# The weights stage of a graph kernel: part of the one-hot work moved to GpSimd

## What is computed

```python
    alpha = leaky_relu(s_src[row] + s_dst[col], 0.2)
    m = maximum(segment_max(alpha, row), 0.0)
    ex = exp(alpha - m[row])
    denom = segment_sum(ex, row) + (E - deg)[:, None] * exp(-m)
    alpha_n = ex / denom[row]
    msg = alpha_n[:, :, None] * h[col]
    out = segment_sum(msg, col, num_segments=N).reshape(N, H * C) + bias
```

## Time and profile before

| | us |
|---|---|
| median of 3 runs | 5210.12 (5208.03 to 5211.01) |
| profiled execution | 5210.29 |
| its span, first to last instruction | 5208.5 |
| weights stage in it, about | 2488 to 2986 |

### The profile page before, as it was taken

How to read it: one execution, slowest core, us unless ns; L and a number is a source line. 1 busy time by engine, 2 the same in 40 slices (tenths; PEclk the granted TensorE clock), 3 DMA queues, 4 the chain that set the end, 5 groups by cost and what they waited for, 6 DMA issues and landing times. The chain is left out here.

```text
span 5208.5 us, 102749 instructions
## 1 busy us (share of the span) xinstructions
PE 3975.9 (76%) x26030; PEld 3300.0 (63%) x26031; DVE 3727.5 (72%) x8186; ACT 3056.9 (59%) x4419; POOL 3139.4 (60%) x3290
## 2 busy tenths in 40 slices
PE   6887888888888888500899977777777777777778
PEld 5776666667666666400788836666666666666666
DVE  9866666666666666449999957777777777777777
ACT  3455555555555455302999966666666666666665
POOL 0277777777777777730000027777777777777774
PEclk9998988988889898755999989999999999999999
DMA  9855555555555544492200086666666666666665
GB/s 388 275 144 130 131 131 132 132 130 132 131 132 132 132 131 133 137 74 8 60 0 0 11 209 146 146 146 145 146 145 146 145 146 145 147 145 146 145 146 135
DMA packets 1157485, 695.20 MB, mean 133 GB/s; under 512 B 923562, under 2 KB 974948, under 8 KB 1157324
## 3 DMA queue, kind: packets, MB, share of 16 engines
q1 hardware_dynamic: 807980, 307.66, 30.5%
q0 software_dynamic: 131424, 275.52, 18.1%
q10 hardware_dynamic: 218048, 111.65, 7.4%
HBM read 542.65 MB, written 145.42 MB: 132 GB/s over the span
## 5 line engine op out<-in xcount | busy, mean ns | idle before, releaser
L1162 POOL DMA_INDIRECT g_q<-q_d,g_aux x1660 | 1571.2, 947 | 1311.0 <-DMA pw<-g_q 805.5
L614 POOL DMA_INDIRECT rec_d<-rec,place x1568 | 1514.6, 966 | 490.8 <-issue 475.9
L1488 PE MATMUL g_hp<-pw,g_mix 128*128 x3328 | 875.9, 386 | 316.2 <-ACT g_mix L1384 310.9
L1499 PE MATMUL g_ap<-g_hid,g_oh 128*128 128x256 f32 x3328 | 876.6, 386 | 137.0 <-DVE agg L1286 131.8
L721 PE MATMUL lk<-tab_sd,low 128*128 128x196 f32 x3136 | 980.2, 397 | 0.0
L1404 ACT ACTIVATE g_hid<-g_q 128x512 f32<-128x512 f32 x832 | 524.0, 630 | 711.1 <-DVE g_q L1272 699.0
L1272 DVE TENSOR_TENSOR g_q<-g_hp,g_q 128x512 f32<-128x512 f32 x832 | 573.8, 690 | 484.4 <-DMA g_q<-q_d,g_aux 350.3
L1488 PEld LDWEIGHTS g_hp<-pw,g_mix 128*128 128x128 f32 x3328 | 616.0, 190 | 473.9 <-issue 398.5
L593 ACT ACTIVATE equal<-rk,minus_two 128x512 bf16<-128x512 f32 x392 | 258.7, 685 | 944.7 <-DMA rec_d<-rec,place 724.0
L1499 PEld LDWEIGHTS g_ap<-g_hid,g_oh 128*128 128x128 f32 x3328 | 595.7, 190 | 286.4 <-issue 219.9
L1286 DVE TENSOR_TENSOR agg<-agg,g_ap 128x256 f32 x1664 | 691.4, 415 | 100.6 <-PE g_ap L1499 38.9
(11 more groups left out here) (265 smaller groups left out, 5164.9 us busy)
## 6 DMA issues: line engine op xcount, KB each, us to landing
low_row<-rows_d SPq DMA_DIRECT2D x392, 256.0 KB
g_ea<-rec_d SPq DMA_DIRECT2D x208, 256.0 KB, 4.6
rec<-in_ea ACTq DMA_DIRECT2D x196, 256.0 KB
rec_d<-pad ACTq DMA_DIRECT2D x49, 936.0 KB, 6.7
hx_row<-rows_d SPq DMA_DIRECT2D x392, 98.0 KB
g_lrow<-low_row_d SPq DMA_DIRECT2D x208, 128.0 KB, 4.4
g_q<-q_d,g_aux POOLq DMA_INDIRECT x1660, 3.0
rec_d<-rec,place POOLq DMA_INDIRECT x1568
```

The lines of the kernel that those rows point to most:

```text
L614: pool.indirect_dma_start(rec_d, bass.IndirectOffsetOnAxis(ap=place[0:n, at, j:j + 1], axis=0), rec[0:n, at, j, :], None).then_inc(s_sc[at ...
L1162: pool.indirect_dma_start(qg[:, par, j, :], None, q_d, bass.IndirectOffsetOnAxis(ap=aux[:, par, j, F_IDX - F_LOW:REC - F_LOW].bitcast(I32) ...
L1488: mm = pe.matmul(hp[u][:, k * HID:(k + 1) * HID], mix[:, par, 2 * u + k, :], pw[:, bass.ds(b[k], 1), :].rearrange("p o f -> p (o f)"), sta ...
L1499: mm = pe.matmul(ap[u % 2][:, k * HID:(k + 1) * HID], oh[:, par, 2 * u + k, :], hid[:, u, k, :], start=True, stop=True)
```

## The change

GpSimd gets a loop in the weights stage. For each group it subtracts, for tiles 0 to 4 (`AWAY = 5`), the high digit from the numbers 0 to 195, in one operation of 5 x 196 elements that writes the difference into `oh_high`. ScalarE then takes the absolute value in place, in one operation without a bias over the five tiles, and then max(0, 1 - x) as before, over five tiles instead of four. VectorE compares tiles 5 to 7 (`COMPARED = 3`). TensorE starts with those three tiles. The wait for a free buffer moves from ScalarE to GpSimd, and ScalarE waits for GpSimd's new semaphore `d_pool`.

```diff
+AWAY, COMPARED = 5, 3
...
-        high_two = halved_bf[:, S:2 * S].rearrange("p (g j s) -> p g j s", j=HG, s=2)
+        high_two = halved_bf[:, S:S + S // G * COMPARED * 2].rearrange("p (g j s) -> p g j s", j=COMPARED, s=2)
...
-                        act.activation(high_two[:, gs, :, :], by_group[:, :, HG:G].unsqueeze(3).to_broadcast([P, SC // G, HG, 2]),
+                        act.activation(high_two[:, gs, :, :], by_group[:, :, AWAY:G].unsqueeze(3).to_broadcast([P, SC // G, COMPARED, 2]),
                                        ACT.Copy).then_inc(s_ld, 1)
...
             @block.gpsimd
             def _(pool):
+                def away(g, at):
+                    if not first(g, 4):
+                        pool.wait_ge(d_acc, g - 3)
+                    pool.tensor_tensor(oh_high[:, at, 0:AWAY, :], row(high_of, P, AWAY, NQ),
+                                       col(high_dst[:, bass.ds(g * G, AWAY)], P, AWAY, NQ), ALU.subtract).then_inc(d_pool, 1)
+
+                pool.wait_ge(s_const, 1)
+                quads(pool, away, NGS)
...
-                    v.tensor_tensor(oh_high[:, at, HG:G, :].rearrange("p j (a s) -> p j a s", s=2),
-                                    high_two[:, bass.ds(g, 1), :, :].rearrange("p o j s -> p (o j) s").unsqueeze(2)
-                                    .to_broadcast([P, HG, NQ // 2, 2]),
-                                    high_of.rearrange("p (a s) -> p a s", s=2).unsqueeze(1).to_broadcast([P, HG, NQ // 2, 2]),
-                                    ALU.is_equal)
+                    to = [P, COMPARED, NQ // 2, 2]
+                    v.tensor_tensor(oh_high[:, at, AWAY:G, :].rearrange("p j (a s) -> p j a s", s=2),
+                                    high_two[:, bass.ds(g, 1), :, :].rearrange("p o j s -> p (o j) s").unsqueeze(2).to_broadcast(to),
+                                    high_of.rearrange("p (a s) -> p a s", s=2).unsqueeze(1).to_broadcast(to), ALU.is_equal)
...
                 def turned_low(g, at):
-                    if not first(g, 4):
-                        act.wait_ge(d_acc, g - 3)
-                    for j in range(HG):
-                        ins = act.activation(oh_high[:, at, j, :], high_of, ACT.Abs, bias=high_dst[:, bass.ds(g * G + j, 1)], scale=-1.0)
-                    ins.then_inc(d_dist, 1)
+                    act.wait_ge(d_pool, g + 1)
+                    to = oh_high[:, at, 0:AWAY, :].rearrange("p j a -> p (j a)")
+                    act.activation(to, to, ACT.Abs).then_inc(d_dist, 1)
                     act.wait_ge(d_dist, g + 1)
-                    act.activation(oh_high[:, at, 0:HG, :], oh_high[:, at, 0:HG, :], ACT.Relu, bias=ones[:, 0:1], scale=-1.0
-                                   ).then_inc(d_lo, 1)
+                    act.activation(to, to, ACT.Relu, bias=ones[:, 0:1], scale=-1.0).then_inc(d_lo, 1)
...
-                    for j in [*range(HG, G), *range(HG)]:
+                    for j in [*range(AWAY, G), *range(AWAY)]:
```

More of the change, by code:

```diff
@@ L1086, in build @@
             d_hi, d_w, d_acc = sem("e_high_ready"), sem("e_weights_ready"), sem("e_multiplied")
+            d_pool = sem("e_differences_ready")
             d_dist, d_lo = sem("e_distances_ready"), sem("e_low_ready")
@@ L1438, in weighted @@
                             mm = pe.matmul(acc[:, 0:NQ], spread[:, at, k * HEADS:(k + 1) * HEADS, :, j].rearrange("p h q -> p (h q)"),
-                                           oh_high[:, at, j, :], start=first(g) and j == HG and k == 0,
-                                           stop=isinstance(g, int) and g == NGS - 1 and j == HG - 1 and k == THREE - 1,
+                                           oh_high[:, at, j, :], start=first(g) and j == AWAY and k == 0,
+                                           stop=isinstance(g, int) and g == NGS - 1 and j == AWAY - 1 and k == THREE - 1,
                                            skip_group_check=True)
```

## The result

The changed kernel took 5522.12 us (median of 4 runs, 5521.01 to 5523.64) against 5210.57 us for the kernel before (4 runs): a ratio of 1.0597, 95% interval 1.0585 to 1.0610.

What follows compares the result with a forecast made beforehand. ScalarE was taken to bound the weights stage at 2.38 us a group, VectorE close behind. Turns of 2.25 plus 2.13 us make 4.38 us, over 208 groups +416 us on 5210: 5626 us, range 5180 to 5760 us.

Steps and rivals of the forecast that it cites:

- What bounds: Weights stage before the change: 208 groups of 2.38 us, bound by ScalarE, with VectorE only 0.03 us behind.
- the sum: Weights stage: VectorE's 2.25 us plus GpSimd's 2.13 us make 4.38 us a group, +416 us, 5626 us.
- the likeliest case: Weights stage: VectorE's three operations and GpSimd's subtraction take turns by whole instructions, 4.38 us a group, 5626 us; chance 0.55.
- The mechanism: Weights stage: VectorE operations with two SBUF inputs and GpSimd's SBUF-reading subtraction share a read interface, each holding the other.
- GpSimd's price: Subtraction of 980 elements a group: 2.13 us, bounded by 0.90 us (one pass) and 2.53 us (three passes).
- The two-pass value: GpSimd's subtraction if the write runs beside its two reads: 1.72 us a group.
- The turnovers: Two handovers of 0.12 us a group between VectorE and GpSimd, counted only in the upper bound of 5.02 us.
- TensorE's clock: Weights stage: TensorE, idle half the time, may be granted 1.2 GHz and need 4.14 us, still under 4.38 us.
- A: Weights stage: VectorE and GpSimd run side by side, VectorE binds at 2.25 us a group, 5183 us; chance 0.22.
- B: Weights stage: side by side, but the subtraction alone takes 2.53 us, over 2.38 us; +31 us, 5241 us; chance 0.05.
- C: Weights stage: turns shorter than an instruction hide about half the subtraction, 3.32 us a group, 5406 us; chance 0.15.
- The signs it named: Stage timeline: large product or its neighbours about 2.1 us longer once a group, period near 4.4 us; otherwise product unchanged, 2.25 us.

Runs made afterwards that it cites:

- the write-only experiment: The changed kernel with GpSimd's subtraction replaced by a memset of the same 980 elements a group, which reads nothing and leaves the weights out: 5182.68 us.

## Why the prediction was right, point by point

*What bounds.* Right. ScalarE was relieved as worked out: 1021 and 1112 ns against 1.02 and 1.12 us. VectorE's compare takes 467 instead of 593 ns, and its three operations without company 2.25 us a group, as the sum had it; the write-only experiment and the last two groups of the stage both show 2.25. GpSimd's turn came on top, as the likeliest case said.

*The mechanism.* Right, and narrower than the rows of before could tell. In the earlier trace rows the two engines hold one another to the end of an instruction; in the earlier trace rows an addition with two SBUF inputs runs undisturbed inside an indirect DMA of GpSimd. The experiments show that a GpSimd memset doesn't touch VectorE's operations with two SBUF inputs and that an operation that reads SBUF does; the addition of the earlier trace rows would fit if that DMA's operation reads no SBUF in this way, which no run shows. Why the copy of the earlier trace rows, with one input, is held was not tried. The conversion that lasted 5.43 us beside a memset is a second such row: an operation of VectorE with one input can be held too, which the turns found here don't cover. *SBUF — State Buffer* of the Trainium skill, section "Who interferes with whom", says just that of VectorE operations with two SBUF inputs. The runs agree with it in the three ways that were tried: beside memsets the three operations kept 1.75, 0.28 and 0.46 us, beside a reading operation the 256-element compare took 1085 ns, and compares with one SBUF input were not held (0.41 and 0.75 us).

*The mis-sized term.* The step that was off is GpSimd's price, taken as 2.13 us, the middle between two and three passes at the rate of a memset. What a group paid is 1.63 us by the periods (3.88 less 2.25 us) and 1.60 us by the compare's length. That is two passes: alone the whole subtraction takes 1.83 us, which leaves no room for a third pass of 0.81 us behind the reads, so the write runs beside them; and 0.23 us of the operation run beside VectorE, so that no fixed part is paid. The difference, 2.13 less 1.63 us, is 0.50 us a group; times 208 that is 104 us, the whole gap between 5626 and 5522 us. The two-pass value that the prediction listed, 1.72 us, would have given 2.25 + 1.72 = 3.97 us a group and about 5541 us. *GPSIMD Engine Reference* of the Trainium skill, section 3.1, led to an estimate of 2.15 us for the operation; its figure is for an addition of float32 numbers. Alone the subtraction measured 1.83 us here, with bf16 and float32 inputs and a bf16 output, and the measurement decides.

*The turnovers* of 0.12 us, put into the range alone, were not paid on top: 2.25 and 1.60 us are 3.85 of the period's 3.88 us. The 0.14 us by which the held compare outlasts the subtraction lie within the 0.28 us that it needs anyway.

*TensorE's clock.* It was granted 1.00, the upper level of 2.4 GHz, in the stretch shown although TensorE was idle for 1.80 us in each group, and the 24 loads kept their 2.07 us. The 4.14 us that the prediction estimated for 1.2 GHz did not come up; they would have bound, since the period is 3.88 us.

*The rivals.* A (side by side, 5183 us) would have needed the subtraction to leave the compares alone; its time is what a GpSimd operation without reads gives, 5182.68 us. B falls with the 1.83 us, which is under 2.38 us. C (half of it hidden, 3.32 us a group) falls with the period of 3.88 us, of which only 0.23 of 1.83 us are hidden, and with the lengths: a compare of 0.28 us waits out 1.6 us of reads, while the product ahead of it is not stretched at all.

*The signs it named.* Two of them were badly chosen. The large product's length was to decide between the likeliest case and A, and the prediction was to be wrong if the product kept its length while a subtraction ran beside it. In the plain stretch it does keep it, 1.75 us, and only at the stage's start one product took 3.37 us. Still the two take turns there: the subtraction starts after the product and waits for it, 3.06 us where it takes 1.83 us alone. By that sign alone the result would have been read as A, or as a miss. What tells the cases apart is the length of the product's neighbour, 1893 ns, which the prediction named too, and the period. The second poor sign is the range: 5180 to 5760 us reaches from a faster kernel to one that is 550 us slower, so that a time inside it says little; the case's own range, 5370 to 5759 us, says more. The other condition was met: the price lies between 0.90 and 2.53 us.

Neither the changed kernel nor the one with its numbers in PSUM, the two that still compute the weights, beats the kernel before. An element that GpSimd reads costs VectorE 0.81 ns, and the subtraction reads two for each; a compare on VectorE costs 0.53 ns an element. So a tile that VectorE gives up gives back 0.10 us and takes 0.32 us (196 x 2 x 0.81 ns), and the four tiles that came from ScalarE give VectorE nothing back. By this estimate, which rests on two and on five tiles, the move loses for any number of tiles, as long as all of VectorE's operations read two streams of SBUF.

## What to carry to other kernels

Before work is moved to an idle GpSimd, look at what VectorE runs meanwhile: where its operations have two inputs in SBUF and no gaps, every element that GpSimd reads is paid in VectorE's time (0.81 ns each here), so that the move pays only if it frees more than that, even if GpSimd has nothing else to do. What GpSimd only wrote cost such operations nothing here, but a memset held a VectorE conversion with one input for its whole 5.33 us, so that writing is not free in general. An engine whose smallest, unchanged operation suddenly takes six times as long, with the end of another engine's instruction just ahead of its own end, is being held and not working: its busy time reads as full either way.

## What the runs showed that was not expected

In these runs the hold goes by the elements read: 632, 790 and 1598 ns for 784, 980 and 1960 elements, with one stream or two. The victim need not be the operation that is long: in the plain stretch it was the one that came next behind the product, 256 elements in size, at the stage's start the other compare and the product, and with one SBUF input in the compares the product alone. 0.23 us of a GpSimd subtraction of 1.83 us don't take part in the turns. And a GpSimd memset that left VectorE's two-input operations alone held a conversion of VectorE with one input.
